# Keys and queries split straight from PSUM, from the tenth projection on

## What is computed

```python
xn = _layernorm(x, axis=-1)
x = x + gnn(xn, W1, b1, W2, b2, eps, src, dst) + mix(xn[None], W_qkv, W_out, b_out)[0]
x = x + ffn(_layernorm(x, axis=-1)[None], ...)[0]

# gnn: neigh = segment_sum(feat[src], dst); rst = (1 + eps) * feat + neigh
#      h = relu(rst @ W1 + b1) @ W2 + b2 + feat
# mix: q, k, v = split(xn @ W_qkv.T) in 8 heads of 64; q *= 64 ** -0.5
#      attn = relu(q @ k.T) @ v   (no softmax); out = attn @ W_out.T + b_out
```

## Time and profile before

| | us |
|---|---|
| median of 3 executions | 762.74 |
| lowest and highest | 760.39, 764.14 |
| the profiled execution | 763.66 |
| its span, first to last instruction | 761.5 |
| mean granted TensorE clock | 0.947 of full speed |
| busy: TensorE matmul | 682.0 (90%) |
| busy: VectorE | 465.7 (61%) |
| busy: ScalarE | 232.2 (30%) |
| busy: GpSimd | 179.9 (24%) |

### The profile page before, as it was taken

One profiled execution on the slowest core, in us unless ns is written; L12 is line 12 of the kernel. 1 busy time (PEld: TensorE's weight loads), 2 busy tenths in 40 slices (PEclk: granted clock), 3 DMA queues, 4 the chain that ended last, 5 costly groups with the idle time before them and its releaser, 6 DMA issues.

```text
span 761.5 us, 12313 instructions
## 1 busy us (share of the span) xinstructions
PE 682.0 (90%) x3840; PEld 452.1 (59%) x3841; DVE 465.7 (61%) x923; ACT 232.2 (30%) x472; POOL 179.9 (24%) x267
## 2 busy tenths in 40 slices
PE   4877999999999999999999999999996398999944
PEld 2544545455555555555555898989883276777600
DVE  5637674479898898797855984254545223333346
ACT  2312211133233233233334333334242044444300
POOL 6056353102123240322101900030311110000064
PEclk9998899999999999999999999999996599999955
DMA  9600000072543707273464900020239685343467
GB/s 296 192 0 0 1 0 3 1 277 75 220 170 124 281 13 279 77 272 113 182 243 168 375 1 0 1 79 6 84 117 422 254 298 173 124 139 123 150 186 232
DMA packets 48902, 109.48 MB, mean 144 GB/s; under 512 B 6842, under 2 KB 6858, under 8 KB 46384
## 3 DMA queue, kind: packets, MB, share of 16 engines
q1 hardware_dynamic: 44480, 92.11, 33.5%
q0 software_dynamic: 4336, 16.41, 6.6%
HBM read 47.35 MB, written 61.16 MB: 142 GB/s over the span
## 4 chain that ended last, share of the span: by engine, by line
PE 73%; DVE 8%; DMA 6%; issue 6%; POOL 4%; ACT 2%; SPq 1%; POOLq 0%; DVEq 0%; ACTq 0%
PE bank L1297 11%; PE bank L1280 10%; PE bank L1216 7%; PE bank L1392 6%; PE bank L1335 6%; PE bank L1458 6%; PE bank L1248 6%; PE bank L1444 6%; PE bank L1259 5%; PE bank L1180 4%; PE bank L1320 4%; DVE arena L896 3%; DMA arena<-slots 2%; DMA arena<-in_x 2%; POOL arena L629 2%
## 5 line engine op out<-in xcount | busy, mean ns | idle before, releaser
L896 DVE TENSOR_TENSOR arena<-iota,arena 125x384 f16<-125x384 f16 (+2 forms) x318 | 186.5, 647 | 23.4 <-PE bank L1180 14.1
L703 ACT ACTIVATE arena<-bank 128x416 f32<-128x416 f32 (+1 forms) x120 | 62.2, 518 | 147.0 <-PE bank L1280 144.0
L1297 PE MATMUL bank<-arena 128*64 128x416 f32 (+1 forms) x480 | 97.2, 524 | 3.2 <-DVE arena L937 2.8
L937 DVE TENSOR_SCALAR arena<-bank 128x416 f32<-128x416 f32 (+1 forms) x120 | 67.4, 586 | 42.9 <-PE bank L1280 42.8
L526 POOL COPY arena<-arena 125x12 f32 (+1 forms) x80 | 35.7, 446 | 198.0 <-DVE arena L896 103.3
L1248 PE MATMUL bank<-arena 128*128 128x416 f32 (+1 forms) x192 | 77.7, 555 | 2.4 <-ACT arena L644 1.4
L1115 DVE COPY arena<-arena 128x1024 f32 x30 | 20.8, 694 | 67.6 <-issue 64.7
L1180 PE MATMUL bank<-arena 125*128 125x160 f16 x471 | 52.0, 235 | 11.3 <-DVE arena L896 10.7
L1180 PEld LDWEIGHTS bank<-arena 125*128 125x128 f16 x471 | 32.3, 98 | 43.4 <-issue 26.6
L1444 PEld LDWEIGHTS bank<-arena 128*128 128x128 f32 x448 | 54.0, 198 | 6.2 <-issue 6.2
L1248 PEld LDWEIGHTS bank<-arena 128*128 128x128 f32 x192 | 37.6, 204 | 30.9 <-issue 27.7
(11 more groups left out here) (227 smaller groups left out, 1173.7 us busy)
## 6 DMA issues: line engine op xcount, KB each, us to landing
slots<-arena SPq DMA_DIRECT2D x6, 5376.0 KB, 17.2
arena<-in_ew SPq DMA_DIRECT2D x11, 1024.0 KB, 15.6
slots<-arena SPq DMA_DIRECT2D x2, 5120.0 KB, 15.8
arena<-slots SPq DMA_DIRECT2D x32, 256.0 KB, 2.8
slots<-arena SPq DMA_DIRECT2D x28, 256.0 KB, 2.0
arena<-in_ew POOLq DMA_DIRECT2D x5, 1024.0 KB, 7.4
arena<-in_x SPq DMA_DIRECT2D x8, 512.0 KB, 7.0
arena<-in_gw SPq DMA_DIRECT2D x2, 2048.0 KB, 17.6
```

Of the source, the lines that this page charges most:

```text
L703: act.activation(probs[0:kt, s % NPB, 0, 0:n], bank[2 * (s % 2)][0:kt, 0:n], ACT.Relu).then_inc(p0_ready, 1)
L896: ins = dve.tensor_tensor(hot[:, :, c], iota16[0:CE, 0:width].unsqueeze(1).to_broadcast([CE, n, width]), window_cols[:, i % WBUF, of, k0:k ...
L937: dve.tensor_single_scalar(probs[0:kt, s % NPB, 1, 0:n], bank[2 * (s % 2) + 1][0:kt, 0:n], 0.0, op=ALU.max).then_inc(p1_ready, 1)
L1297: ins = pe.matmul(bank[AV][DH * a:DH * a + DH, 0:n], v_sb[0:kt, t, h * DH:h * DH + DH], probs[0:kt, s % NPB, a, 0:n], start=(t == 0), stop ...
```

## The change

From projection 9 on (`RAW = 9`, the first query block of pair 1) the split is made from the PSUM bank. ScalarE writes the rounded part directly to `k_hi` or `q_hi`, and VectorE, in turn g + 1, writes the remainder from the bank and the rounded part to `k_lo` or `q_lo`, in one `scalar_tensor_tensor`. GpSimd keeps the splits of pair 0 and of k of pair 1; the latter's place in its list moves from 12.5 to 9.5. TensorE waits for the remainder as well before it writes a bank again, and ahead of the value projections. The waits of the scores follow the splits that are left.

```diff
@@ -281,7 +281,7 @@
         qk_ps, p0_ready, p1_ready, av_step, av_saved = (
             sem(s) for s in ("qk_ps", "p0_ready", "p1_ready", "av_step", "av_saved"))
         v_saved = sem("v_saved")
-        q_split, k_split = sem("q_split"), sem("k_split")
+        q_split, k_split, proj_rest = sem("q_split"), sem("k_split"), sem("proj_rest")
         out_ps, out_added = sem("out_ps"), sem("out_added")
         w2_hi_ready, w2_lo_ready = sem("w2_hi_ready"), sem("w2_lo_ready")
         wo_hi_ready, wo_lo_ready, o_hi_ready = (sem(n) for n in ("wo_hi_ready", "wo_lo_ready", "o_hi_ready"))
@@ -326,6 +326,7 @@
 
         NPRE = NPROJ + NT
         HIGH_FROM = 8
+        RAW = 9
         PREP, FROM, EARLY = 4, 8, 16
         EVERY = 1.675
         pe_after, act_after, dve_after = ([[] for _ in range(NPRE + NS)] for _ in range(3))
@@ -508,8 +509,8 @@
             pool.sem_inc(zeros_ready, 1)
             def split_pair(p):
 
-                pool.wait_ge(proj_saved, 6 * (p + 1))
-                for hi, lo, of, ready in ((k_hi, k_lo, k_t, k_split), (q_hi, q_lo, q_t, q_split)):
+                pool.wait_ge(proj_saved, min(6 * (p + 1), RAW))
+                for hi, lo, of, ready in ((k_hi, k_lo, k_t, k_split), (q_hi, q_lo, q_t, q_split))[:2 - p]:
                     link(pool.tensor_copy(hi[p][:, :], of[:, p, :]))
                     link(pool.tensor_tensor(lo[p][:, :], of[:, p, :], hi[p][:, :].bitcast(f32), ALU.subtract))
                     pool.sem_inc(ready, 1)
@@ -581,7 +582,7 @@
                     pool.sem_inc(spare_waited, 1)
 
             for _, what, i in sorted([(start(max(w - 4, 0)), "cols", w) for w in range(NW)]
-                                     + [(6 * (p + 1) + 0.5, "split", p) for p in range(PAIRS)]
+                                     + [(min(6 * (p + 1), RAW) + 0.5, "split", p) for p in range(2)]
                                      + [(summed[w // WPG], "spare", w) for w in range(0, NW, 2)]):
                 {"cols": window_columns, "spare": spare_chunks, "split": split_pair}[what](i)
 
@@ -669,7 +670,10 @@
                     if t in (1, 3):
                         deviation(t // 2 + 2)
                 act.wait_ge(proj_ps, g + 1)
-                if which == "k":
+                if g >= RAW:
+                    hi, scale = (k_hi, 1.0) if which == "k" else (q_hi, SCALE)
+                    act.activation(hi[p][:, o:o + n], bank[g % 5][:, 0:n], copy, scale=scale).then_inc(proj_saved, 1)
+                elif which == "k":
                     act.activation(k_t[:, p, o:o + n], bank[g % 5][:, 0:n], copy).then_inc(proj_saved, 1)
                 else:
                     act.activation(q_t[:, p, o:o + n], bank[g % 5][:, 0:n], copy, scale=SCALE).then_inc(proj_saved, 1)
@@ -908,7 +912,19 @@
                                              in1=rst, op0=ALU.mult, op1=ALU.add).then_inc(rst_ready, 1)
 
 
+            def keep_projection_rest(g):
+
+                which, p, b = projections[g]
+                o, n = BLOCKS[b]
+                hi, lo, scale = (k_hi, k_lo, 1.0) if which == "k" else (q_hi, q_lo, SCALE)
+                dve.wait_ge(proj_saved, g + 1)
+                dve.scalar_tensor_tensor(out=lo[p][:, o:o + n], in0=bank[g % 5][:, 0:n], scalar=scale,
+                                         in1=hi[p][:, o:o + n].bitcast(f32), op0=ALU.mult,
+                                         op1=ALU.subtract).then_inc(proj_rest, 1)
+
             for turn in range(FROM, NPRE):
+                if RAW < turn <= NPROJ:
+                    keep_projection_rest(turn - 1)
                 if HIGH_FROM < turn <= HIGH_FROM + NT:
                     t = turn - HIGH_FROM - 1
                     dve.wait_ge(xn_stored, 16)
@@ -1244,13 +1260,15 @@
                     pe.wait_ge(consts_ready, 2)
                 if g >= 5:
                     pe.wait_ge(proj_saved, g - 4)
+                if g - 5 >= RAW:
+                    pe.wait_ge(proj_rest, g - 4 - RAW)
                 for k in range(KD):
                     ins = pe.matmul(bank[g % 5][:, 0:n], w_qkv[:, part, k, c:c + P], xn_t[:, k, o:o + n],
                                     start=(k == 0), stop=(k == KD - 1))
                 ins.then_inc(proj_ps, 1)
                 lay_out_edges(g - PREP)
                 graph(g)
-            pe.wait_ge(proj_saved, NPROJ)
+            pe.wait_ge(proj_rest, NPROJ - RAW)
             pe.wait_ge(wv_in, 16)
             for t in range(NT):
                 if t >= 5:
@@ -1271,8 +1289,8 @@
                     pe.wait_ge(p0_ready, s - 1)
                     pe.wait_ge(p1_ready, s - 1)
                 if s % (len(BLOCKS) * NT) == 0:
-                    pe.wait_ge(k_split, p + 1)
-                    pe.wait_ge(q_split, p + 1)
+                    pe.wait_ge(k_split, min(p + 1, 2))
+                    pe.wait_ge(q_split, 1)
                 terms = ((k_hi, q_hi), (k_hi, q_lo), (k_lo, q_hi))
                 for i, (k, q) in enumerate(terms):
                     for a in range(2):
```

## The result

The changed kernel took 755.7 us (median of 4, 753.89 to 756.49), the kernel before beside it 763.44. The ratio is 0.990, 95% interval 0.987 to 0.993. The forecast was 755.0 with 752.0 to 760.5, and a sum of 8.2 us; the medians differ by 7.7, and so do the spans of the profiled executions, 761.5 and 753.8.

A forecast was written before the change was run, and what follows sets the result against it. TensorE was taken to bound the kernel, losing time only where it stands still or runs slowly. 7.3 + 1.7 - 0.8 = 8.2 us off gave 755.5, or 754.5 from the median; forecast 755.0, whole range 752 to 760.5.

The forecast's parts named there:

- Place (b): Projections 13 to 15: GpSimd's split of pair 1 holds VectorE, TensorE stands, then runs slowly; 7.3 us to be regained.
- Place (c): Projections 19 to 23: GpSimd's split of pair 2 holds VectorE, without a clock fall; 1.7 us to be regained.
- The last wait: Ahead of the value projections: TensorE now waits for remainder 23 and starts about 0.8 us later.
- Sum: Whole kernel: 7.3 + 1.7 - 0.8 = 8.2 us gained.
- ScalarE's saves at no cost: Projection stage: fifteen saves write the rounded part instead of a plain copy, 0.518 us against 0.52; cost nothing.
- Remainders at 0.59: Projection stage: VectorE's fifteen added remainders take 0.59 us each, 8.9 us in all, covered by its idle time.
- the margin at turn 12: Projection 12 and its window pairs: VectorE's one-hots done 0.1 us before TensorE wants them, the tightest margin.
- The k split ahead of its old place: GpSimd's k split of pair 1: cast 60.2 to 61.4, subtraction 61.5 to 64.7 us, stretching one xn_lo.
- (a): Behind projection 9: TensorE waits until 54.91 us; pair 0 is split as before, so this stays.
- Projections 10 to 23 in even steps: Projection stage, sign of being right: steps of 3.1 us, projection 15 near 73.2 and 23 near 97.9.
- rival 4: More than forecast: slow-clock turns 10 and 11, or later pairs, gain as well; 752 or less, chance 0.07.
- the 0.5 us that I set aside for a held remainder: Turns 11 and 12: if remainder 10 were held too, TensorE would stand about 0.5 us, gain 7.7 instead of 8.2.

The follow-up runs named there:

- raw12: Changed kernel with RAW = 12, both halves of pair 1 split by GpSimd again at the old place; 766.41 us, ratio 1.005 to the kernel before.
- lo_set: Kernel before with GpSimd's four subtractions for pairs 1 and 2 each replaced by two memsets to zero; 758.48 us.
- rest_twice: Changed kernel with each of VectorE's fifteen remainders made twice; 757.39 us, ratio 0.992 to the kernel before.
- raw6_again: Changed kernel with RAW = 6, k of pair 1 split from PSUM too, run again for its trace; 757.84 us in one timing.
- late_all: Kernel before with all four GpSimd splits placed later in its list, nothing split from PSUM; 749.45 us, ratio 0.983.
- late_two: Changed kernel with the two splits GpSimd keeps moved to turns 24.5 and 27.5 in its list; 756.05 us, ratio 0.992 to the kernel before.
- rest_four: Changed kernel with each of VectorE's remainders made four times; 773.29 us.
- v_only: Changed kernel with value projections waiting only for the remainder of their own bank; 753.38 us, ratio 0.987 to the kernel before.

## Why the prediction was right

- **Place (b), 7.3 us.** 13.47 us became 6.23: 7.24. raw12 brings it back (13.16, 0.3 short of before, with projection 14 at 5.29 us for 5.61), lo_set takes it away without any PSUM split.
- **Place (c), 1.7 us.** 14.04 became 12.40: 1.64.
- **The last wait, -0.8 us.** 3.61 became 4.24: -0.63. The term had 0.13 for VectorE's start behind ScalarE's end and was rounded up; here VectorE starts 0.03 behind it (102.29 to 102.32), and its 0.59 is the rest.
- **Sum** 8.25 against 8.2. The medians differ by 7.7. In the traces behind the stage +1.5 us ahead of the expert loop and -1.8 in it cancel, which is luck: the forecast had no term for either.
- **ScalarE's saves at no cost.** 0.518 us as k_hi and q_hi, as before.
- **Remainders at 0.59.** 0.578 to 0.595 us, fifteen of them. As an occupation they are 0.5 to 0.6: the term was a little too high, as were the other durations in VectorE's turn. It made margins look tighter than they were, and rest_twice dearer than it was. It didn't touch the sum. About half of what the margin at turn 12 gained (0.7 us for 0.1) comes from it; the other half is that GpSimd's subtraction took 2.83 us for 3.15 and ended 0.4 us sooner than in my layout.
- **The k split ahead of its old place.** Forecast 60.2 to 64.7, in this execution 60.96 to 65.10, with the stage 0.8 late; the stretched xn_lo was there. It costs nothing (raw6_again).
- **"(a) stays".** True of this change. What I hadn't asked is why GpSimd must split pair 0 first: nothing reads that split before the scores at 154 us. late_all got 6.7 us more for a changed sort key.
- **"Projections 10 to 23 in even steps".** True from 11 on. Turn 10 stayed at 4.8 us, at the lower clock behind (a), so rival 4's first place gained nothing.

The Trainium skill, "SBUF — State Buffer", section "Who interferes with whom", says that a VectorE instruction with at most one SBUF input, outside certain fast modes, doesn't contend with GpSimd, and that one with two contends only with a GpSimd instruction that reads SBUF. The runs agree on both: the remainder of 84.94 keeps 0.59 us in the middle of a subtraction, and the four one-hots beside lo_set's memsets take 2.15 us together, as they do alone. So the 0.5 us that I set aside for a held remainder wasn't needed.

## What to carry to other kernels

An engine with time to spare can still set the pace of another, through what its instructions exclude while they run: line up long GpSimd instructions that read SBUF with VectorE's two-input ones, and look at single durations, not means. Before moving such work to another engine, ask when its result is first needed and whether it can run where the held engine has slack; here that was worth nearly twice the rewrite. Ask too what stands behind it in its list: at (a) the loss was VectorE waiting for work queued behind a split. An earlier or later place in an in-order list is only an order, so a delay that matters needs a wait.

## What the runs showed of the hardware

- One-input VectorE reads with the other operand in PSUM run beside GpSimd's SBUF reads without loss (0.59 us), while the two-input ones are held to the end of the instruction (2.98 us for 0.69). The one that starts first holds the other: a cast that started 0.02 us behind an xn_lo took 1.74 us for 1.23 (lo_set).
- GpSimd instructions that only write SBUF (memsets, 1.2 us each) don't hold VectorE; casts of the same length do.
- Behind a standstill of 3.7 us (late_two) or 3.3 us (before, raw12) the granted clock fell (0.67 in late_two's stretch above, 0.57 before) to its lower level, 1.2 GHz, for most of the next projection, which then took 6.38 us for 3.64 (late_two), 5.61 (before) or 5.29 (raw12) for 3.00. In rest_four, with standstills of 0.2 to 1.4 us in nearly every turn, projections kept 3.0 us; behind its last one, 5.47 us, value projection 0 took 6.12.
- The clock can also differ between executions at the same place of the same code: 0.83 in changed and 1.00 in v_only in the two stretches shown above, both with TensorE busy for 10.00 of 10 us.
- In back-to-back VectorE work the start-to-start step is 0.05 to 0.1 us shorter than the recorded duration; a sum over an engine's turn should use steps.
